# A causal attention block with feed-forward: half of the probability tiles turned on TensorE instead of by VectorE and DMA

## What is computed

```python
q, k, v = heads(x @ Wq), heads(x @ Wkv[:, :1024]), heads(x @ Wkv[:, 1024:])
s = einsum('bhid,bhjd->bhij', q * 64 ** -0.5, k)
p = where(causal_mask, 0, exp(s - max(s, axis=-1)))      # row maximum over all 1024 keys
out = einsum('bhij,bhjd->bhid', p, v) / (sum(p, -1) + 1e-8)
x = layernorm(x + out_of_all_heads @ Wo + bo)
xr, xk = mu_r * x + (1 - mu_r) * x_prev, mu_k * x + (1 - mu_k) * x_prev
x = layernorm(x + sigmoid(xr @ W_r.T) * (relu(xk @ W_k.T) ** 2 @ W_v.T))
```

## Time and profile before

| | us |
|---|---|
| median of 3 runs (lowest, highest) | 1599.26 (1597.0, 1601.52) |
| the profiled execution's own time | 1593.41 |
| its span, first to last instruction | 1591.6 |
| TensorE products busy | 1068.9 (67%) |
| VectorE busy | 1026.8 (65%) |
| ScalarE busy | 658.4 (41%) |
| GpSimd busy | 572.8 (36%) |
| mean granted TensorE clock | 0.880 of 2.4 GHz |

### The profile page before, as it was taken

One profiled execution on the slowest core, in us unless ns is written; L12 is line 12 of the kernel. 1 busy time (PEld: TensorE's weight loads), 2 busy tenths in 40 slices (PEclk: granted clock), 3 DMA queues, 4 the chain that ended last, 5 costly groups with the idle time before them and its releaser, 6 DMA issues.

```text
span 1591.6 us, 21533 instructions
## 1 busy us (share of the span) xinstructions
PE 1068.9 (67%) x6771; PEld 659.7 (41%) x6771; DVE 1026.8 (65%) x1844; ACT 658.4 (41%) x1442; POOL 572.8 (36%) x904
## 2 busy tenths in 40 slices
PE   6677667676766666776676667666666766666474
PEld 4444434444434444443444444344444434434252
DVE  6667666566766666676666667666666766666467
ACT  4344434344444434443443444334344433433244
POOL 5243334333433433343343334334333433432110
PEclk9899898979989897898889899889899989897787
DMA  4554555556455555544556564455555555555601
GB/s 129 135 129 110 123 124 127 128 137 138 112 114 127 124 130 133 136 115 114 129 119 132 134 135 115 114 125 126 128 135 136 116 112 127 125 127 136 136 14 40
DMA packets 319955, 192.82 MB, mean 121 GB/s; under 512 B 108768, under 2 KB 315360, under 8 KB 319840
## 3 DMA queue, kind: packets, MB, share of 16 engines
q1 hardware_dynamic: 319264, 191.05, 52.2%
q10 hardware_dynamic: 576, 0.39, 0.1%
HBM read 21.17 MB, written 2.36 MB: 15 GB/s over the span
## 4 chain that ended last, share of the span: by engine, by line
SPq 81%; issue 7%; DMA 5%; DVE 3%; PE 3%; ACT 0%; POOL 0%; DVEq 0%; ACTq 0%
SPq L274 79%; DMA recips<-recips_sb 4%; SPq L286 2%; PE ps_x L751 1%; DMA pt<-stage 1%; DVE stats L571 1%; PE ps_s L715 1%; DVE pt L593 0%; DVE tile L582 0%; DVE y L582 0%; DMA pt<-in_L_attn_x 0%; DVE tile L637 0%; PE ps_x L654 0%; DVE tile L634 0%; DVE pt L626 0%
## 5 line engine op out<-in xcount | busy, mean ns | idle before, releaser
L432 ACT ACTIVATE tile<-tile,neg_max 128x640 f32<-128x640 f32 (+7 forms) x512 | 396.6, 775 | 790.3 <-POOL tile L340 790.0
L545 DVE TENSOR_SCALAR_CACHE_REDUCE tile<-ps_s 128x1024 f32<-128x1024 f32 x512 | 600.6, 1208 | 75.8 <-PE ps_s L715 75.8
L556 DVE STREAM_TRANSPOSE stage<-tile 128x640 f32<-128x640 f32 (+7 forms) x512 | 365.6, 752 | 436.7 <-DMA pt<-stage 436.7
L751 PE MATMUL ps_x<-pt,vs 128*64 128x256 f32 (+1 forms) x2560 | 355.8, 431 | 323.5 <-DMA pt<-stage 323.0
L715 PE MATMUL ps_s<-ks,qs 64*128 64x512 f32 x3072 | 449.7, 426 | 158.5 <-DVE tile L545 156.0
L340 POOL TENSOR_SCALAR_AFFINE_SELECT tile<-tile 128x128 f32<-128x128 f32 x512 | 150.4, 294 | 896.7 <-DVE tile L545 896.5
L715 PEld LDWEIGHTS ps_s<-ks,qs 64*128 64x128 f32 x3072 | 290.3, 196 | 320.9 <-DVE tile L545 198.8
L751 PEld LDWEIGHTS ps_x<-pt,vs 128*64 128x64 f32 x2560 | 198.9, 160 | 483.1 <-DMA pt<-stage 357.4
L654 PE MATMUL ps_x<-xs,ws 128*128 128x512 f32 x381 | 121.1, 427 | 0.0
L347 POOL TENSOR_TENSOR ot<-ot,rb 128x512 f32<-128x512 f32 x64 | 101.2, 1581 | 41.3 <-ACT ot L455 24.9
L432 ACT ACTIVATION_READ_ACCUMULATOR tile<-tile,neg_max 128x1 f32 x512 | 95.8, 187 | 0.0
(11 more groups left out here) (69 smaller groups left out, 371.8 us busy)
## 6 DMA issues: line engine op xcount, KB each, us to landing
pt<-stage SPq DMA_DIRECT2D x512, 128.0 KB, 3.4
pt<-stage SPq DMA_DIRECT2D x512, 96.0 KB, 2.2
pt<-stage SPq DMA_DIRECT2D x512, 64.0 KB, 2.1
pt<-stage SPq DMA_DIRECT2D x512, 32.0 KB, 2.0
rb<-recips SPq DMA_DIRECT2D x64, 256.0 KB, 4.1
out<-y SPq DMA_DIRECT2D x4, 512.0 KB, 3.2
y<-in_L_attn_x SPq DMA_DIRECT2D x3, 512.0 KB, 8.6
pt<-in_L_attn_Wkv SPq DMA_DIRECT2D x2, 384.0 KB, 7.1
```

Of the source, the lines that this page charges most:

```text
L432: act.activation(cols, cols, ACT.Exp, bias=neg_max[:, at:at + 1], scale=-1.0, accum_out=sums[:, p % 2, a, t:t + 1]).then_inc(s_exp, 1)
L545: dve.tensor_scalar(tile[:, at, :], ps_s[scores_at(p, t, a)][:, :], -SCALE, None, ALU.mult, ALU.min, accum_out=neg_max[:, at:at + 1]).then ...
L556: dve.transpose(stage_unit(u)[:, 2 * a + t % 2, :, 0:32 * (t + 1)], tile[:, slot_of(p, t, a), 0:(t + 1) * P].rearrange("p (j b k) -> p b j ...
L751: ins = mm(bank[a * DH:(a + 1) * DH, cols + second * P:cols + 2 * P], vs[:, p // 2 % 2, j, p % 2, a * DH:(a + 1) * DH], moving, start=(j = ...
```

## The change

Tiles 0 to 3, units 0 and 1, are turned by TensorE: `turn_tile` on TensorE multiplies each 128x128 block by the identity into a shared bank, one step after the tile's own, and ScalarE's `take_turned` copies it into the same places of `pt`. Tiles 4 to 7 (`BLOCKWISE`) are turned as before. The P*V products move: units 0 and 1 together in step 7 of their own pair, unit 2 in step 5 and unit 3 in step 6 of the next pair. There are two score places (`NSCORES` 3 to 2) and four shared banks (`NSHARED` 2 to 4) in the same PSUM. One q/k projection stands in each of steps 0 to 3, the v projections in 0 and 1, the output projections in step 4 (first half) and step 0 of the pair after (second half). The three reciprocal transfers are issued by ScalarE: the first after the exponentials of step 0, the others after those of step 1.

```diff
+BLOCKWISE = range(TILES // 2, TILES)
+TURNED_IN = {0: ((0, 1),), 1: ((0, 1),), 2: ((0,), (1,)), 3: ((0,), (1,))}
-QK_AT = {1: (0, 1), 3: (2,), 6: (3,)}
-SPLIT_AT = {1: 0, 2: 1, 4: 2, 6: 3}
-V_AT = {1: 0, 3: 1}
+QK_AT = {0: 0, 1: 1, 2: 2, 3: 3}
+SPLIT_AT = {1: 0, 2: 1, 3: 2, 4: 3}
+V_AT = {0: 0, 1: 1}
+TURN_AT = {1: 0, 2: 1, 3: 2, 4: 3}
-OUT_AT = {6: 0, 7: 1}
-NORM_AT = {3: 0, 5: 1}
-PV_AT = {0: ((0, 0, (0, 1)), (0, 1, (0, 1, 2, 3))), 2: ((1, 2, (0, 1, 2, 3, 4, 5)),),
-         4: ((2, 3, (0, 1, 2, 3)),), 5: ((2, 3, (4, 5, 6, 7)),)}
+OUT0_AT = 4
-NSCORES = 3
-NSHARED = 2
+NSCORES = 2
+NSHARED = 4
...
@@ block.sync
-                at_least(sp, s_pv, 3 * (p - 1) + PV_DONE[u])
-                sp.wait_ge(s_turned, SLOTS * p + 4 * u + 4)
+                at_least(sp, s_pv, 3 * (p - 1) + u)
+                sp.wait_ge(s_turned, 8 * p + 4 * (u - 2) + 4)
...
-            for p in range(ALL_PAIRS + 1):
-                if p > 0:
-                    spread_recips(p - 1)
-                    move(p - 1, 3)
-                if p < ALL_PAIRS:
-                    for u in range(3):
-                        move(p, u)
+            for p in range(ALL_PAIRS):
+                move(p, 2)
+                move(p, 3)
@@ block.gpsimd
+                    if t == 7 and 0 < p <= ALL_PAIRS:
+                        norm(p - 1, 1)
                     if p < ALL_PAIRS:
                         mask(p, t, 0)
                         mask(p, t, 1)
...
+                    if t == 3 and 0 < p <= ALL_PAIRS:
+                        norm(p - 1, 0)
...
@@ block.scalar
+            def take_turned(p, t, n):
+                heads = TURNED_IN[t][n]
+                bank = ps_x[BANK["quad", p, t, n]][:, :]
+                at_least(act, s_pv, 3 * (p - 1) + 1)
+                act.wait_ge(s_quad, 8 * p + 2 * t + heads[-1] + 1)
+                if t == 0:
+                    act.activation(pt_unit(0)[:, 0::2, :, 0:32],
+                                   bank[:, 0:2 * P].rearrange("p (x a i) -> p x a i", x=2, a=4), ACT.Copy
+                                   ).then_inc(s_pt, 1)
+                    return
+                for m, a in enumerate(heads):
+                    cols = bank[:, m * (t + 1) * P:(m + 1) * (t + 1) * P].rearrange("p (j a i) -> p j a i", a=4, i=32)
+                    place = pt_unit(t // 2)[:, 2 * a + t % 2, :, 0:32 * (t + 1)].rearrange("p a (j i) -> p j a i", i=32)
+                    act.activation(place, cols, ACT.Copy).then_inc(s_pt, 1)
+            def column_recips(p):
+                act.wait_ge(s_recip, p + 1)
+                at_least(act, s_rb, 32 * (p - 1))
+                act.dma_start(r_dram[p % 2, :, :].rearrange("a (p t) -> p a t", p=P),
+                              recips[:, p % 2, :, :]).then_inc(s_rdram, 16)
+            def spread_recips(p):
+                act.wait_ge(s_rdram, 16 * (p + 1))
+                at_least(act, s_norm, 2 * p)
+                for a in range(2):
+                    act.dma_start(rb[a * DH:(a + 1) * DH, :], r_dram[p % 2, a, :].partition_broadcast(DH)
+                                  ).then_inc(s_rb, 16)
...
@@ block.vector
+                q, u = (p, t - 2) if t >= 2 else (p - 1, t + TILES - 2)
+                if u in BLOCKWISE:
+                    at_least(dve, s_turned, 8 * q + 2 * (u - 4) + a + 1)
+                else:
+                    dve.wait_ge(s_quad, 8 * q + 2 * u + a + 1)
...
-                    if 0 <= q < ALL_PAIRS:
+                    if 0 <= q < ALL_PAIRS and u in BLOCKWISE:
                         turn_tile(q, u, 0)
                         turn_tile(q, u, 1)
@@ block.tensor
+            def turn_tile(p, t, n):
+                unit = ("quad", p, t, n)
+                heads = TURNED_IN[t][n]
+                drained(unit)
+                for m, a in enumerate(heads):
+                    pe.wait_ge(s_exp, SLOTS * p + 2 * t + a + 1)
+                    for j in range(t + 1):
+                        at = (m * (t + 1) + j) * P
+                        ins = turn(ps_x[BANK[unit]][:, at:at + P], tile[:, slot_of(p, t, a), j * P:(j + 1) * P],
+                                   ident[:, :])
+                    ins.then_inc(s_quad, 1)
...
+                    if t == 5 and p > 0:
+                        values(p - 1, 1, (2,))
+                    if t == 6 and p > 0:
+                        values(p - 1, 2, (3,))
+                    if t == 7 and p < ALL_PAIRS:
+                        values(p, 0, (0, 1))
```

## The result

The changed kernel takes 1244.08 us (median of 4 runs, 1243.71 to 1244.47) against 1599.12 before: a ratio of 0.7779, 95% interval 0.7766 to 0.7793. I had said 1277 and a range from 1245 to 1345.

A forecast was written before the change was run, and what follows sets the result against it. SyncE's issuing of block transfers was taken as the bound. Start 14.4, first pair 36, 31 pairs of 36.2 (1122.2), last transfers 20.2 and tail 78 gave 1270.8; run corrections made it 1277 us, range 1245 to 1345.

The forecast's parts named there:

- The bound before: Kernel before: SyncE's issuing of 64 block transfers per pair, 0.67 us each, sets the 46.4 us pair, not the bytes.
- The loop, 4.23 us: With two score places, scores and both evacuations of a step wait for each other; no step can be shorter than 4.23 us.
- The sum over the pair, 36.2 us: Eight steps of a pair of heads sum to 36.0 us, plus 0.2 for unplaced waits.
- Steps 0 and 1 together: Start of a pair: 4.62 us for step 0, set by TensorE, and 4.92 for step 1, set by VectorE.
- The 0.2 for waits that I could not place: Per pair: 0.2 us added to 36.0 for waits of a tenth here and there.
- The other terms: Outside the 31 pairs: first scores at 14.4 us, first pair 36, last transfers 20.2, the rest to the end 78.
- my one rival below the forecast: Steps hide more: without the added 0.2 and tile 7's spill, 35.3 us a pair and 1249 us; chance 0.10.
- the spill of tile 7: VectorE's turn of tile 7 runs on into step 1, which then lasts 4.92 us instead of 4.23.
- ScalarE: Seven added copies (3.3 to 5.5 us) and three DMA issues per pair leave it 25 to 28 us busy in 36; no cost.
- The shared banks: Four PSUM banks instead of two, 17 users per pair instead of 11; waits for copies cost nothing.
- The clock: TensorE keeps full clock except in the first pair; the opposing low-clock case, up to 1990 us, had chance 0.03.
- The rule on issuing engines: Trainium skill: several issuing engines save only sequencer time, usually small; read as time staying near 1599 us, contradicted by the trace.

## Why the prediction was right in its mechanism and wrong in its size

**The bound before: right.** It was the number of SyncE's issues; with 64 issues per pair the 42.7 us came back, with 48 it did not matter.

**The loop, 4.23 us: right.** Steps 2 to 4 measured 4.21 to 4.22. Shorter evacuations shortened them as worked out (0.52 for 0.54 us), and a third place shortened steps 2 and 3.

**The sum over the pair, 36.2 us: too high; it measured 35.26, and this is the step that failed.** Four terms made the difference.

Steps 0 and 1 together: 9.54 against 9.13. They are VectorE's chain, and I had it too long. "Tile 6 therefore puts off the evacuation of step 0 by about 0.2" is the largest part, 0.25 in the sum: it puts it off by nothing. The turn starts 0.23 us ahead of the scores (649.06 and 649.29), not 0.06, and the evacuation follows 2.02 after its start, not 2.10, so it starts 1.79 after the scores like any other. The remaining 0.16 comes from adding rows of VectorE with their full length, where the next one starts earlier. From the first evacuation of step 0 to the end of the last of step 1 I had 7.44 and the trace has 7.28. The rows before would have given it, 840.00 to 847.28:

```profile
840.00 1.19 DVE L545 TENSOR_SCALAR_CACHE_REDUCE tile<-ps_s 128x1024 f32<-128x1024 f32 x1
...
847.20 0.08 DVE L545 DVE_READ_ACCUMULATOR tile<-ps_s 128x1 f32 x1
```

How the 9.54 was split, 4.62 for step 0 and 4.92 for step 1 (measured 4.19 and 4.94), had no part in it. TensorE's 4.56 for step 0 was too long as well, its own work there is 4.05, but VectorE's chain would have taken up any gain.

Step 5: 4.3 against 4.20. Step 6: 5.15 against 4.98. Both were sums of rows of TensorE, as if each occupied it for its whole length. But the scores last 1.65 and the next product starts 1.58 later, the 32 records of P*V last 3.46 and the next scores start 3.39 later. From start to start TensorE's work in step 5 is 4.10, as long as the step took with the shorter evacuations, so the loop sets it and not TensorE. The overlap could be seen before: with the row

```profile
844.59 0.86 PE L654 MATMUL ps_x<-xs,ws 128*128 128x512 f32 x3
```

a q/k and a v projection take 844.59 - 842.84 = 1.75, where their durations give 1.93.

The 0.2 for waits that I could not place: they were not there. Steps 2 to 4 were 12.69 against 12.64.

Step 7, 4.3 against 4.31, is right by luck. I had it as TensorE's work, but TensorE waited 0.34 us there for VectorE; it is a step of the loop with 0.1 more, for which I have no cause. Over 31 pairs the whole makes 1122.2 against 1096.0.

**The other terms.** These rows of the changed kernel give them (first scores; first scores of the second pair; output projection right behind the last pair's P*V; P*V of the last unit):

```profile
14.30 1.66 PE L757 MATMUL ps_s<-ks,qs 64*128 64x512 f32 x12 [1.94 <-DVE qs L565]
...
49.12 1.67 PE L757 MATMUL ps_s<-ks,qs 64*128 64x512 f32 x12
...
1145.11 1.12 PE L818 MATMUL ps_x<-ot,wos 128*128 128x512 f32 x2
...
1166.57 5.15 PE L807 MATMUL ps_x<-pt,vs 128*64 128x256 f32 x32 [3.25 <-DMA pt<-stage]
```

The first pair took 34.8 us (I said 36), 31 pairs 1096.0 (1122.2), the last transfers 21.5 (20.2), the rest 76.1 (78): 1242.7 against 1270.8. Besides, I added 4.4 us because the profiled run before lay 0.37% below its median. That was scatter of single runs, not a ratio to carry over: the profiled run after, 1244.47, is the highest of its four, 0.03% above their median. Without it the forecast was 1272.6.

**The range: wrong at its lower end, and for a reason that I could have seen.** It began at 1245 because my one rival below the forecast took away the 0.2 and the spill of tile 7. Its numbers, 35.3 us a pair and 1249, came close by luck: the spill of tile 7 is real (step 1 took 4.94, not 4.23). What I had no rival for was that my sums counted the overlap of neighbouring rows twice, and that tile 6 would not spill.

**ScalarE: right.** No cost, with the copies at 0.38 to 0.60 us by width, that is, the lower bound; 2.4 us more of ScalarE's time per pair also cost nothing.

**The shared banks: right in the cost, but I did not ask what they were worth.** I took four banks as harmless and the two places as given. The runs say that the exchange of a score place for two shared banks costs 95 us of the possible gain, while with two places two shared banks do as well as four.

**The clock: right.** The granted clock was 1.00 from the first to the last reciprocal transfer (54.1 to 1147.8 us), with stops of up to 1.3 us in steps 1 to 4 and 7. Between the same two transfers before, where arriving transfers stopped TensorE for several microseconds at a time (5.9 in one wait of the pair of the earlier trace rows), it was 0.88. The first pair shows the low level: after two stops of 2.56 us ahead of the scores of steps 6 and 7 the clock was 0.59 from 44 to 46 us, 0.55 from 46 to 48, with TensorE at work all the time, and 1.00 again from 48 to 50. The Trainium skill ("TensorE: Matmul & The Clock Gate", section "What's actually happening") names activity as what releases the throttle, and the trace agrees. The rest in five steps of a pair was not enough to lose it.

**The rule on issuing engines: misread.** I set the issue time beside itself ("0.67 of 0.67"). Beside one transfer's way from issue to landing, 2.0 to 3.4 us before by size, it is a fifth to a third. Nor does the rule keep the time near 1599: half of the transfers were not moved to another queue but left out.

## What to carry to other kernels

A queue that only issues transfers can be the bound: count its issues and multiply by the distance of their starts, and moving work off it pays only until the next loop is met. Sum an engine's work from start to start of neighbouring rows, never from their durations, and ask of each step which engine's chain ends last: where another's does, an error in the first has no price. When a resource such as PSUM is divided anew, price both sides apart: here the third score place was worth some 93 us and two more shared banks nothing.

## What was not expected of the hardware

Issuing a transfer of 512 bytes took SyncE 0.66 us, hardly less than the 0.68 us of one with 96 or 128 KB. ScalarE's copy out of PSUM into blocks of 32 elements took 0.60 us for 512 columns, as a copy into plain rows did, and 0.38 us for 256, against 0.36.
